# The second norm taken from the first variance in closed form, in the token-shift stage and the expert stage

## What is computed

```python
def _layernorm(x, axis=-1, eps=1e-05):
    m = jnp.mean(x, axis=axis, keepdims=True)
    v = jnp.var(x, axis=axis, keepdims=True)
    return (x - m) / jnp.sqrt(v + eps)
...
        def _rmsnorm(x, w, eps=1e-06):
            inv = jax.lax.rsqrt(jnp.mean(x * x, axis=-1, keepdims=True) + eps)
            return x * inv * w
...
    h = h + _L3_attn_ref(_layernorm(h, axis=-1), ...)
    h = h + _L3_ffn_ref(_layernorm(h, axis=-1), ...)
```

## Time and profile before

| | us |
|---|---|
| median of 3 runs | 5131.06 (5128.0 to 5135.81) |
| span of the profiled execution | 5202.0 |
| TensorE busy | 4518.9 (87%) |
| VectorE busy | 3442.4 (66%) |
| GpSimd busy | 2384.8 (46%) |
| ScalarE busy | 2164.4 (42%) |
| matmuls of L2993 and L3061, 2048 each | 439.3 and 400.7 |

### The profile page before, as it was taken

One profiled execution on the slowest core, in us unless ns is written; L12 is line 12 of the kernel. 1 busy time (PEld: TensorE's weight loads), 2 busy tenths in 40 slices (PEclk: granted clock), 3 DMA queues, 4 the chain that ended last, 5 costly groups with the idle time before them and its releaser, 6 DMA issues. The chain is left out here.

```text
span 5202.0 us, 64516 instructions
## 1 busy us (share of the span) xinstructions
PE 4518.9 (87%) x22312; PEld 2888.0 (56%) x22312; DVE 3442.4 (66%) x7100; ACT 2164.4 (42%) x4039; POOL 2384.8 (46%) x1510
## 2 busy tenths in 40 slices
PE   7888599858888888888887899797899899999999
PEld 4555267633333333333332455596444799999998
DVE  3764222258898998988988323211886788888885
ACT  3654011125555555555555223232664233333332
POOL 3442400169999999999999000000122123222332
PEclk8998799979999999999998899898999899999999
DMA  2003113322222222222222000374000200000000
GB/s 72 1 1 113 60 60 116 120 72 69 69 69 72 69 69 69 69 71 70 69 69 65 17 1 7 123 267 155 1 0 1 87 3 5 5 5 5 5 5 5
DMA packets 153108, 287.18 MB, mean 55 GB/s; under 512 B 24441, under 2 KB 135024, under 8 KB 144206
## 3 DMA queue, kind: packets, MB, share of 16 engines
q1 hardware_dynamic: 144926, 263.59, 15.5%
q0 software_dynamic: 6656, 14.04, 0.9%
q10 hardware_dynamic: 1200, 5.42, 0.3%
HBM read 252.33 MB, written 33.42 MB: 55 GB/s over the span
## 5 line engine op out<-in xcount | busy, mean ns | idle before, releaser
L1509 PE MATMUL ssm_ps<-ssm_hc,net_ident 128*128 128x452 f32 x2048 | 961.5, 596 | 191.6 <-DVE ssm_hc L1765 105.9
L1691 POOL TENSOR_TENSOR ssm_dBu<-ssm_du,ssm_bc 128x904 f32<-128x904 f32 x512 | 1066.5, 2107 | 3.2 <-POOL ssm_du L1709 1.7
L1610 ACT ACTIVATE ssm_ps<-ssm_step,ssm_decay 128x448 f32<-128x448 f32 x1024 | 647.5, 636 | 646.9 <-DVE ssm_ps L1755 435.4
L1509 PEld LDWEIGHTS ssm_ps<-ssm_hc,net_ident 128*128 128x128 f32 x2048 | 392.5, 204 | 727.7 <-issue 347.1
L1755 DVE TENSOR_TENSOR_SCAN ssm_ps<-ssm_ps,ssm_dBu 128x452 f32<-128x452 f32 x512 | 565.0, 1104 | 131.6 <-ACT ssm_ps L1610 45.2
L1755 DVE TENSOR_TENSOR_SCAN ssm_hs<-ssm_ps,ssm_dBu 128x452 f32<-128x452 f32 x512 | 551.2, 1077 | 41.5 <-ACT ssm_ps L1610 35.0
L1702 POOL TENSOR_TENSOR ssm_hc<-ssm_hs,ssm_bc 128x904 f32<-128x904 f32 x256 | 539.2, 2106 | 74.2 <-DVE ssm_hs L1755 74.1
L3135 POOL TENSOR_TENSOR peer_hid<-peer_hid,peer_weight 128x452 f32<-128x452 f32 x256 | 294.1, 1188 | 525.0 <-ACT peer_weight L3082 525.0
L2993 PE MATMUL peer_ps<-peer_xn,peer_down 128*128 128x226 f32 x2048 | 439.3, 361 | 0.0
L3061 PE MATMUL peer_ps<-peer_hid,peer_up 128*128 128x226 f32 x2048 | 400.7, 354 | 3.1 <-POOL peer_hid L3135 2.2
L3061 PEld LDWEIGHTS peer_ps<-peer_hid,peer_up 128*128 128x128 f32 x2048 | 386.4, 189 | 12.9 <-POOL peer_hid L3135 6.2
(11 more groups left out here) (424 smaller groups left out, 7871.0 us busy)
## 6 DMA issues: line engine op xcount, KB each, us to landing
ssm_bc<-ssm_rows SPq DMA_DIRECT2D x256, 452.0 KB, 3.6
ex_w<-in_l_ffn_w SPq DMA_DIRECT2D x64, 1024.0 KB, 6.6
moe_w_gu<-in_moe_gate_up SPq DMA_DIRECT2D x16, 704.0 KB
slots_in<-rt_zeros SPq DMA_DIRECT2D x17, 640.0 KB, 8.7
moe_rows_in<-slots_in SPq DMA_DIRECT2D x16, 512.0 KB
slots_out<-xp_rows_out SPq DMA_DIRECT2D x16, 512.0 KB
moe_w_dn<-in_moe_down SPq DMA_DIRECT2D x16, 384.0 KB
peer_down<-in_peer_down_t SPq DMA_DIRECT2D x1, 4096.0 KB, 16.6
```

Of the source, the lines that this page charges most:

```text
L1509: nc.tensor.matmul(Y_BANK[j][:, 0:GT], c["ident"][:, :], hc[:, q % 2, j, :], start=False, stop=(n == S - 1))\
L1610: nc.scalar.activation(rows(dA(i % 2))[:, :, lo:lo + N - 1], rows(step[hf.d][:, j, :])[:, :, lo:lo + N - 1], ACT.Exp, scale=decay[hf.d][:, ...
L1691: nc.gpsimd.tensor_tensor(dBu[:, q % 2, j:j + 2, :], du[hf.d][:, j:j + 2, :], bc[:, q % RING, 0:1, :].to_broadcast([P, 2, GT]), ALU.mult). ...
```

## The change

The input of the second norm is itself a layer norm, so its mean is zero and its variance is v / (v + eps), where v is the variance of the residual. Both roots together are therefore one function of v: (1 + eps) v + eps^2 under the root in the token-shift stage, and (1 + 1e-6) v + 1e-6 * 1e-5 in the expert stage. In the token-shift stage `root_again` takes Ln and Exp of this from the same PSUM bank right behind the roots of norm 0, and `norm_again` multiplies the centred input by it; the mean, centring, square, variance and roots of norm 1 are gone. In the expert stage `inverse_root` takes the one root, `scaled_input` scales the centred input by it, and the first scaling, the second square, `second_moment` and the second Ln and Exp are gone. The next centring now waits until the readers of the centred input are done. The diff, cut to the changed lines:

```diff
@@ -2310,9 +2311,10 @@
         x = st.sbuf("x", [P, 2, DK, GT])
-        norms = [Norm(st, ps[0], ps[0], "ln0", out=x)]
-        norms.append(Norm(st, ps[0], ps[0], "ln1", square=norms[0].square))
-        norms.append(Norm(st, ps[1], ps[1], "ln2"))
+        norms = {0: Norm(st, ps[0], ps[0], "ln0", out=x), 2: Norm(st, ps[1], ps[1], "ln2")}
+        log_again, rstd_again = (st.sbuf(f"{x_}_again", [P, GT]) for x_ in ("log", "rstd"))
+        eps_again = st.sbuf("eps_again", [P, 1])
+        normed_again = st.sbuf("normed_again", [P, DK, GT])
@@ -2349,6 +2351,7 @@
             def _(pool):
+                nc.gpsimd.memset(eps_again[:, :], LN_EPS * LN_EPS)
@@ -2383,9 +2386,6 @@
             def _(pe):
-                def mean(j, g, ap):
-                    norms[j].tensor_mean(nc, pe, c["ones"], ap)
-
@@ -2432,7 +2432,7 @@
                         if early:
-                            pe.wait_ge(norms[1].log_ready, early)
+                            pe.wait_ge(s["log_again_done"], early)
@@ -2445,15 +2445,8 @@
                         hidden(late_, 3)
-                    if live(early):
-                        pe.wait_ge(norms[0].ready, early + 1)
-                        norms[1].tensor_mean(nc, pe, c["ones"], lambda k: x[:, early % 2, k, :])
-                    if live(late_):
...
-                    if live(early):
-                        norms[1].tensor_var(nc, pe, c["ones"], early + 1)
-                    if live(late_):
@@ -2489,10 +2482,20 @@
                     act.wait_ge(norms[j].centred_ready, g + 1)
-                    if j == 0 and g:
-                        act.wait_ge(norms[1].var_ready, g)
+                    if g:
+                        act.wait_ge(norms[j].var_ready, g)
...
+                def root_again(g):
...
+                    nc.scalar.activation(log_again[:, :], ps[0][:, 0:GT], ACT.Ln, bias=eps_again[:, 0:1], scale=1.0 + LN_EPS)\
+                        .then_inc(s["log_again_done"], 1)
+                    act.wait_ge(s["log_again_done"], g + 1)
+                    if g:
+                        act.wait_ge(s["again_done"], g)
+                    nc.scalar.activation(rstd_again[:, :], log_again[:, :], ACT.Exp, scale=-0.5).then_inc(s["rstd_again_done"], 1)
@@ -2549,6 +2552,7 @@
                         norms[0].scalar_root(nc, act, c["eps"], early + 1)
+                        root_again(early)
@@ -2558,8 +2562,6 @@
                         weights(mid, 0)
-                    if live(early):
-                        squares(1, early)
@@ -2568,8 +2570,6 @@
                     nc.scalar.preload_act_table_set(EXP_LN)
-                    if live(early):
-                        norms[1].scalar_root(nc, act, c["eps"], early + 1)
@@ -2609,6 +2609,8 @@
                         dve.wait_ge(norms[j].ready, g)
+                    if j == 0 and g:
+                        dve.wait_ge(s["again_done"], g)
@@ -2621,12 +2623,19 @@
-                def scaled(g, norm, dst, gain, bias, done, free, count):
-                    dve.wait_ge(norm.ready, g + 1)
+                def norm_again(g):
+                    dve.wait_ge(norms[0].centred_ready, g + 1)
+                    dve.wait_ge(s["rstd_again_done"], g + 1)
+                    nc.vector.tensor_tensor(normed_again[:, :, :], norms[0].centred[:, :, :],
+                                            rstd_again[:, :].unsqueeze(1).to_broadcast([P, DK, GT]), ALU.mult)\
+                        .then_inc(s["again_done"], 1)
...
+                def scaled(g, ready, src, dst, gain, bias, done, free, count):
+                    dve.wait_ge(ready, g + 1)
...
-                        nc.vector.tensor_scalar(dst[:, k, :], norm.out[:, k, :], col[:, gain, k:k + 1],
+                        nc.vector.tensor_scalar(dst[:, k, :], src[:, k, :], col[:, gain, k:k + 1],
@@ -2754,9 +2763,6 @@
                         lags(mid, 1)
-                    if live(early):
-                        dve.wait_ge(norms[0].ready, early + 1)
-                        centre(1, early, x[:, early % 2, :, :])
@@ -2768,8 +2774,8 @@
                             dve.wait_ge(s["h1_done"], DK * early)
-                        norms[1].vector_scale(nc, dve, early + 1)
-                        scaled(early, norms[1], h1, G1, B1, s["h1_done"], s["mix_done"], DK * 3 * early)
+                        norm_again(early)
+                        scaled(early, s["again_done"], normed_again, h1, G1, B1, s["h1_done"], s["mix_done"], DK * 3 * early)
@@ -2786,7 +2792,7 @@
                         norms[2].vector_scale(nc, dve, mid + 1)
-                        scaled(mid, norms[2], h2, G2, B2, s["h2_done"], s["mix2_done"], 2 * DK * mid)
+                        scaled(mid, norms[2].ready, norms[2].out, h2, G2, B2, s["h2_done"], s["mix2_done"], 2 * DK * mid)
@@ -2815,11 +2821,10 @@
         ramp = st.sbuf("ramp", [P, P])
-        eps6 = st.sbuf("eps6", [P, 1])
-        norm = Norm(st, ps[0], ps[0], "ln", PT)
-        log2, rms = norm.log_var, norm.rstd
+        eps_both = st.sbuf("eps_both", [P, 1])
...
-        names = ("sq2", "ms_mm", "log2_done", "rms_done", "xn_done", "sim_mm", "top_done", "idx_done", "pair_done", "best_done", "at_done",
+        norm = Norm(st, ps[0], ps[0], "ln", PT, out=xn)
+        names = ("xn_done", "sim_mm", "top_done", "idx_done", "pair_done", "best_done", "at_done",
@@ -2827,27 +2832,24 @@
-        def second_moment(pe, k):
-            pe.wait_ge(s["sq2"], k + 1)
+        def inverse_root(act, k):
...
+            act.wait_ge(norm.centred_ready, k + 1)
+            nc.scalar.activation(norm.square[:, :, :], norm.centred[:, :, :], ACT.Square).then_inc(norm.square_ready, 1)
+            act.wait_ge(norm.var_ready, k + 1)
+            nc.scalar.activation(norm.log_var[:, :], ps[0][:, 0:PT], ACT.Ln, bias=eps_both[:, 0:1], scale=1.0 + RMS_EPS)\
+                .then_inc(norm.log_ready, 1)
+            act.wait_ge(norm.log_ready, k + 1)
+            nc.scalar.activation(norm.rstd[:, :], norm.log_var[:, :], ACT.Exp, scale=-0.5).then_inc(norm.rstd_ready, 1)
...
+        def scaled_input(dve, normed):
...
+            dve.wait_ge(norm.centred_ready, normed)
+            dve.wait_ge(norm.rstd_ready, normed)
...
-                mm = nc.tensor.matmul(ps[0][:, 0:PT], c["ones"][:, :], norm.square[:, m, :], start=(m == 0), stop=(m == DK - 1))
-            mm.then_inc(s["ms_mm"], 1)
-
-        def root_mean_square(act, k):
-            act.wait_ge(norm.ready, k + 1)
-            nc.scalar.activation(norm.square[:, :, :], norm.out[:, :, :], ACT.Square).then_inc(s["sq2"], 1)
-            act.wait_ge(s["ms_mm"], k + 1)
-            nc.scalar.activation(log2[:, :], ps[0][:, 0:PT], ACT.Ln, bias=eps6[:, 0:1]).then_inc(s["log2_done"], 1)
-            act.wait_ge(s["log2_done"], k + 1)
-            nc.scalar.activation(rms[:, :], log2[:, :], ACT.Exp, scale=-0.5).then_inc(s["rms_done"], 1)
-
-        def scaled_input(dve, normed):
-
-            dve.wait_ge(norm.ready, normed)
-            dve.wait_ge(s["rms_done"], normed)
-            for m in range(DK):
-                nc.vector.scalar_tensor_tensor(out=xn[:, m, :], in0=norm.out[:, m, :], scalar=nw[:, m:m + 1],
-                                               in1=rms[:, :], op0=ALU.mult, op1=ALU.mult).then_inc(s["xn_done"], 1)
+                nc.vector.scalar_tensor_tensor(out=xn[:, m, :], in0=norm.centred[:, m, :], scalar=nw[:, m:m + 1],
+                                               in1=norm.rstd[:, :], op0=ALU.mult, op1=ALU.mult).then_inc(s["xn_done"], 1)
@@ -2882,12 +2884,10 @@
-        def best_experts(dve, k, normed):
+        def best_experts(dve, k):
...
-                if b and normed is not None:
-                    norm.vector_scale(nc, dve, normed)
@@ -3021,14 +3021,12 @@
                     norm.tensor_var(nc, pe, c["ones"], 1)
-                    second_moment(pe, 0)
-                    pe.wait_ge(s["log2_done"], 1)
+                    pe.wait_ge(norm.log_ready, 1)
...
-                    second_moment(pe, 1)
@@ -3046,7 +3044,7 @@
                         if afters[k] is not None:
-                            pe.wait_ge(s["log2_done"], k + 2)
+                            pe.wait_ge(norm.log_ready, k + 2)
@@ -3061,8 +3059,6 @@
                             mm.then_inc(s["up_mm"], 1)
-                            if afters[k] is not None and m == 0:
-                                second_moment(pe, k + 2)
@@ -3089,11 +3085,9 @@
                     nc.scalar.preload_act_table_set(EXP_LN)
+                    act.wait_ge(set_, 2)
...
-                        norm.scalar(nc, act, c["eps"], i + 1)
-                        if i == 0:
-                            act.wait_ge(set_, 2)
-                        root_mean_square(act, i)
+                        inverse_root(act, i)
@@ -3110,14 +3104,13 @@
                             nc.scalar.preload_act_table_set(EXP_LN)
-                            norm.scalar(nc, act, c["eps"], k + 3)
-                            root_mean_square(act, k + 2)
```

(12 more changed lines are left out.)

3 lines of the change are left out of this document (2 added, 1 removed).

## The result

| | before | after |
|---|---|---|
| median of 5 runs, us | 5131.06 | 5097.77 (5091.39 to 5100.32) |
| ratio | | 0.9934 (95% interval 0.9922 to 0.9946) |
| span of the profiled execution | 5202.0 | 5095.6 (its time: 5097.33) |
| token-shift stage, first mean of `h` to the expert stage's | 425.87 | 402.41 |
| expert stage, from there to the end of the span | 1168.96 | 1157.86 |

The kernel became 33.3 us faster, 0.66%; forecast were 39.1 us and a time of 5092. In the two profiled executions the stages that the change touches gave 23.5 and 11.1 us, 34.6 together, which agrees with the medians. The spans differ by 106 us, but 72 us of that lie ahead of the token-shift stage, in work that the change doesn't touch: in the execution of before the stage's first load was issued at 3593.56 us, in that of after at 3521.94.

The account below looks back on a forecast made before the run. The prediction took TensorE to set the pace of both stages. Token-shift stage 27.2 us (9.6 + 0.8 + 16.8) plus expert stage 11.9 us gave 39.1 us, from 5131.06 to 5092 us, range 5084 to 5108.

Parts of the forecast that it names:

- likeliest case: Whole kernel: the forecast of 5092 us, own range 5086 to 5098, chance 0.60.
- What bounds the kernel: Both stages: TensorE sets the pace, busy 46.01 of 47.00 us in token-shift windows and 69.00 of 69.00 in the expert stage.
- Iteration 0 and 1: Token-shift stage's first two iterations: 9.6 us from the dropped second scaling chain, 0.8 us from VectorE's lost subtraction.
- Full iterations, 2.8 us each: Token-shift iterations 2 to 7: TensorE reaches the third norm's mean 2.8 us earlier each, 16.8 us in all.
- VectorE is then 1.5 us ahead: Full token-shift iterations: the removed subtraction and less waiting outweigh the 0.6 us late Ln, leaving VectorE 1.5 us earlier.
- lie beside L2733 and L2735: Full token-shift iterations: GpSimd's squares now run beside these VectorE instructions; 904 elements take 1.84 instead of 1.10 us.
- The removal of the matmuls on TensorE: Full token-shift iterations: eight matmuls for mean and variance go, 3.03 us of TensorE per iteration.
- Expert stage, 11.9 us: Expert stage: 14 steps lose 0.76 us of weight loads each, 10.6 us, plus 1.3 us in the prologue.
- The prologue: Start of the expert stage: 1.3 us less, range 0 to 3, as key products then wait for the weights.
- Hand-offs keep most of it: Full token-shift iterations: VectorE's order bounds them, only its subtraction counts, 6.6 us instead of 16.8; 5102 us, chance 0.13.
- The port rule: Full token-shift iterations: VectorE and GpSimd block each other on a shared port, 1.9 us saved each; 5097 us, chance 0.12.
- Clock: Full token-shift iterations: added pauses drop TensorE to 1.2 GHz, some 40 us per fallen iteration; 5172 us, chance 0.04.

Follow-up runs that it names:

- e9: The changed kernel run again, unedited, beside the kernel before: 5100.16 us, ratio 0.9942.
- e5: Changed kernel with the eight removed matmuls given back to TensorE alone, their result read by nobody: 5106.76 us, full iteration 45.98 us.
- e3: Changed kernel with the moved Ln and Exp issued behind the Ln of the sums instead of ahead: 5100.23 us, full iteration 44.45 us.
- e6: Changed kernel with the squares of hidden blocks 6 and 7 made by ScalarE instead of GpSimd: 5092.2 us, full iteration 43.66 us.
- e7: Changed kernel with GpSimd's squares of hidden blocks 2 and 3 cut to 1 of 452 columns, leaving work out: 5097.66 us, full iteration 44.45 us.
- e8: Changed kernel with Ln and Exp behind the Ln of the sums and squares of blocks 6 and 7 on ScalarE: 5089.68 us, full iteration 43.22 us.
- e4: Changed kernel with one unused subtraction of the removed shape given back to VectorE in iterations 1 to 7: 5110.9 us, ratio 0.9955.

## Why the prediction was right, and where it was not

The time, 5097.77, lies at the upper edge of the likeliest case's own range (5086 to 5098), 5.8 us over the forecast. That it lies inside is partly luck: the same kernel came out at 5100.16 in e9. Step by step:

**What bounds the kernel**: right for the expert stage, where the 0.76 us of weight loads came off each step to the hundredth. For the token-shift stage "TensorE sets the pace" was true of before only with 1.7 us of room to VectorE; after the change both end together, and e5 shows that 3.03 us of TensorE's queue are worth 1.08.

**Iteration 0 and 1**: right. The second scaling chain fell out whole (9.8 of 9.6 forecast), and iteration 1 lost the subtraction and gained the late Ln (0.7 of 0.8, with a stretch at the lower clock in it before and after; in e9, without that stretch, it gained 2.25).

**Full iterations, 2.8 us each**: the term that was mis-sized; it is 2.12. The failed step is "VectorE is then 1.5 us ahead". The ledger of VectorE from its first scaling to the end of the sum: before 3877.57 to 3897.12, 19.55 us; after 3652.05 to 3671.05, 19.00 us. Out went the subtraction with its wait (1.09 + 0.81) and a wait of 0.36 for ScalarE; in came 0.51 for the late Ln. That makes 1.75, and 0.55 is what came. The other 1.2 is GpSimd. In both traces some of VectorE's instructions are 0.62 to 0.74 us longer than their twins (instructions of the same line or shape with no square beside them); each of them began while a square ran. Before there were four of these ahead of the end of the sum:

```profile
3881.17 0.63 DVE L2698 TENSOR_TENSOR rw_s<-rw_PPp,rw_kp 128x452 f32<-128x452 f32 x1
3881.83 1.02 DVE L2701 TENSOR_SCALAR rw_d<-rw_s 128x452 f32<-128x452 f32 x1
...
3887.09 0.63 DVE L2708 TENSOR_TENSOR rw_d<-rw_d,rw_v 128x452 f32<-128x452 f32 x1 [0.36 <-ACT rw_d L2520]
3887.76 1.72 DVE L2711 TENSOR_TENSOR_SCAN rw_aa<-rw_d 128x452 f32<-128x452 f32 x1
3889.40 1.37 DVE L2718 COPY rw_AAp<-rw_aa 128x452 f32<-128x452 f32 x2
```

(These are L2701, the second scan L2711 and the two copies L2718; the fourth is L2735: 0.62 + 0.62 + 0.70 + 0.74 = 2.7 us. The row at 3887.09 holds the wait of 0.36 us.) After there are six: L2707, L2710, L2717, the second scan L2720, L2742 and L2744, 3.9 us. I had put this at 0.3 us, and said only that the squares would "lie beside L2733 and L2735". That the late Ln pushes the second lag under the squares of blocks 2 and 3 I had not seen, nor that this would delay ScalarE's exponentials, the relu of block 4 and so hidden block 6 by 0.64 us (16 records of hidden blocks 2 to 5 at 0.38 us end at 3659.68, block 6 began at 3660.32). Nor had I carried the same price to the other side: GpSimd's squares of blocks 6 and 7 went from 2.69 to 3.25 us, so that TensorE's last pair was ready late too. The removal of the matmuls on TensorE was sized right; what it was worth was not, because the sum and the last squares came 0.6 us later than forecast, and 0.1 us came behind the mean. e3, e6 and e7 take these collisions away in part, and e8 takes away 1.68 us with two edits; that is more than the 0.7 us that were missing.

**Expert stage, 11.9 us**: 11.1. The 14 steps gave 10.6 as forecast. The prologue was to give 1.3 and gave 0.3 by the first step's mean, with e9 even a loss of 2.0: the key products did start when the last weights landed, and the similarities 1.4 us earlier, but the clock didn't return earlier with them (29.9 us behind the stage's first mean before, 29.7 after), so they ran at the lower level for 3.0 us instead of 1.8 and ended only 0.8 us earlier. I had priced the wait for the copy, and had taken an earlier start for an equally earlier end.

**Rivals**: "Hand-offs keep most of it" has its mechanism in part: VectorE's order does bound the iteration (e4: one to one). But it gave 2.12 and not 1.1 us an iteration, since VectorE was 1.7 us ahead to begin with. The port rule: its 1.9 us an iteration and 5097 us are the nearest of all numbers given. That is close partly by luck, since the total also lacks 0.8 us in the expert stage, which the rule doesn't touch. I had set it aside because L2735 took 1.84 us where I worked out 2.3 by the rule. That was my own sizing: I took half of a row of two squares (2.69 us) for the length of the square. The first of the two took 0.94 us and the second 1.79.

Square by square the rule can be checked. L2707 began at 3656.26 with 0.77 us of a square to go and was 0.62 longer than alone; L2710 began at 3657.55 with 0.86 us to go and was 0.71 longer; L2735 of before had 0.89 us to go and was 0.74 longer. In the token-shift stage of the two profiles 80 instructions of L2707's, L2710's, the scan's and L2735's shapes began while a square ran (34 before, 46 after), and each was longer by what the square still had to go less 0.14 to 0.15 us, the one with only 0.52 us to go (3873.28 us, after) by 0.38. Those that were running when a square began kept their length within 0.03 us, and it was the square that became longer, up to 1.79 us where one that met nothing took 0.94. So each engine waits for the instruction of the other that began first, and they don't slow each other in proportion. The Trainium skill, SBUF — State Buffer, section Who interferes with whom, says that whoever issues first gets the shared ports for the whole instruction and the other blocks fully. The trace agrees: with the square's real length the rule gives 1.10 + 0.89 = 1.99 us for L2735, and 1.84 was seen.

**Clock**: it didn't fall in the changed kernel's full iterations (1.00). It fell in iteration 8 of e9, for 3.4 us, and not in the same iteration of after, though TensorE waited 2.6 us there in both; I had used iteration 8 of before, which kept 1.00, as the argument that it wouldn't. It does fall in three full iterations of e4, at 1.7 us each. The rival's mechanism is real and its price was some twenty times too high.

## What to carry to other kernels

When a matmul is taken out of a full queue, compare the ends that meet at the next join first: here 3.03 us of TensorE work were worth 1.1 us, since VectorE's sum had been only 1.7 us ahead. And when a change moves VectorE's instructions against GpSimd's, count the collisions before and after, from the twins of one line with different lengths: each cost 0.62 to 0.74 us here, and the profile shows it as a longer instruction and not as a wait. Work for GpSimd that stands beside a critical stretch of VectorE is worth moving to an engine that has room, even at a price there (a square took 0.62 us on ScalarE in e6).

## What was not expected of the hardware

- The price of meeting a GpSimd square (128 x 452, float32) on VectorE does not depend on VectorE's instruction: 0.40 became 1.11, 0.63 became 1.25, 1.10 became 1.72. It is what the square still has to go, less 0.14 to 0.15 us; that it is nearly the same each time comes from the two queues running in step. Also an instruction with one tile as its input (L2710) pays it.
- TensorE's clock fell behind a wait of 1.06 us in an iteration in which it was busy for 40.60 of 43.00 us, in iterations 5 to 7 and not in 2 to 4, whose waits are as long, and was back after 3.4 us. What sets the one apart from the other stays open.
- How soon the clock returns in the expert stage's prologue differs between executions of one program (29.7 and 33.0 us behind the stage's first mean): the similarities took 8.60 and 10.05 us.
